# Cross attention of a decoder layer: the value product on the high and low halves of the softmax weights side by side

## The chip, the cores and the metric

The kernel runs on one core of one Trainium2 chip. The metric is the device time in microseconds (us), the median of several runs. TensorE is the matrix engine, VectorE the vector engine, ScalarE the scalar engine, GpSimd (POOL) the fourth, and SyncE (SP) issues the DMAs. In the profile they are PE, DVE, ACT, POOL and SP.

## The reference

One decoder layer on x (8 batches of 224 rows and 512 columns) and a context (8 x 750 x 384). Each of its three parts is followed by a layernorm of x plus the part's output:

```python
x = _layernorm(x + _L0_attn_ref(x, ...))           # self attention, 16 heads of 64, tanh soft clamp
x = _layernorm(x + _L0_xattn_ref(x, ctx_768, ...)) # cross attention
x = _layernorm(x + _L0_ffn_ref(x, ...))            # ternary weights, 8-bit activations

# _L0_xattn_ref, HEADS = 16, DIM_HEAD = 64
q = split_heads(x @ Wq); k = split_heads(context @ Wk); v = split_heads(context @ Wv)
sim = jnp.einsum('bhid,bhjd->bhij', q, k) * SCALE
attn = jax.nn.softmax(sim, axis=-1)
out = jnp.einsum('bhij,bhjd->bhid', attn, v)
out = out.transpose(0, 2, 1, 3).reshape(b, sq, HEADS * DIM_HEAD)
return out @ Wo + bo
```

The change concerns `out = attn x v` of the cross attention: for each batch and head, a product over 750 keys of 224 rows of weights and 64 columns of values.

## The kernel before, in words

**Precision by halves.** Matmuls of float32 data run on fp32r operands. Each operand is split into a high half (the value rounded to fp32r) and a low half (the rest, value minus high), and a product is summed from high x high, high x low and low x high.

**Tiling of the cross attention.** The 16 heads go in two groups of eight (GROUPS = 2). For each group the 8 batches follow one another, so there are 16 steps. In a step the queries (Q0 to Q3) and keys (K00 to K31) are projected for pairs of heads and the values (V00 to V15) for four heads at a time, from the transposed x (XT) and context (CT). For a head h, S are the scores of 112 rows by 750 keys (two heads side by side in banks SA and SB), M the row maxima (DVE, L1618), the exponentials with their row sums (ACT, L1509), R the reciprocals of the sums (DVE, L1623) and N the normalisation of the weights (POOL, L1243).

**From weights to values.** transpose_weights (T, L1392) brings the normalised weights of a head into bank T by three groups of four transposes, so that keys lie on the partitions: six key blocks of 126 (one of 120). For each group weights_hi (ACT, L1515) writes the high half into big_hi, and weights_split (DVE, L1628) the low half into big_lo; the latter frees bank T. weights_view is the place of a group in these tiles, [key, head parity, key block, row]. v_st holds the values of a head as 128 columns, 64 high and 64 low, in an order that changes with the parity of the head.

values (O, L1407) then adds up a head's output in bank O. For each of the six key blocks it runs two products with the same stationary operand, v_st: one with big_hi and one with big_lo as the moving operand, 224 columns each, all twelve into the same 224 columns of the bank. So 64 partitions of the bank hold high values times both halves, and the other 64 hold low values times both halves. lower_values (ACT, L1522) copies the 64 partitions of the low values to the others' place in tmp, and add_values (DVE, L1637) adds the two into o32 and frees the bank. Two heads fill one o32 pair (the even one the first 64 partitions, the odd one the rest). split_output on POOL splits the pair into o_hi (L1248) and o_lo (L1250), and project_out (Y0 and Y1, L1418) multiplies with Wo, after all eight heads. It waits for o_split of pair p before its product 3p+1 of Y0.

**What sets the order.** Each engine works through a list written out by hand (ORDER in tensor, scalar, vector and gpsimd) in which an item with a "+" belongs to the next batch. The engines meet at semaphores: `filled` of a bank is raised by TensorE, `drained` by the last reader. In the stretch around O of TensorE's list: "T3.1 CT01+ O2 T3.2 CT02+ CT10+ S3.0 T4.0 CT11+ O3 T4.1 V00+ V01+ T4.2", and at the turn of the step "T1.1 K30+ K31+ O0+ S2.0+ T1.2 V11+ V12+ T2.0+ V13+ V14+". VectorE's list has there "M6.0 T4.0 CT11+ M7.0 O3 T4.1 R6.0" and "Y1 finish T1.1 K30+ O0+ K31+ M4.0+ T1.2 V11+ M5.0+ V12+"; finish is the bias in the first group and the layernorm in the second. POOL's list has B0 to B3 (split_output of a pair) among the N and the pieces FR, FC and FT of the feed-forward weights, of which FR waits for a DMA. The last step has lists of its own, and further banks (END_UNITS).

Of the kernel before, what the change touches and what calls it, by code (L numbers as in the profile page):

```python
# [14 lines left out]
ALU = mybir.AluOpType  # L15
ACT = mybir.ActivationFunctionType
AX = mybir.AxisListType
F32 = mybir.dt.float32
F32R = mybir.dt.float32r
# [3 lines left out]
P = 128  # L23
BANK = 512
HALF = 64
# [49 lines left out]
def f32(ap):  # L75
    return ap.bitcast(F32)
# [797 lines left out]
def cross_attention(nc, ctx_mem, mem, psum, shared, sa_free, sa_projected, sa_stage_free, ff_scaled, x1, ctx, Wq, Wk, Wv, Wo, bo, acc, x2, ff_held, ff_weights, ff_ternary, ff_scale):  # L874

    B, N, DM = x1.shape
# [4 lines left out]
    NP = HG // 2  # L881
    GC = HG * D
    KC, CC = DM // P, CD // P
    R = N // 2
    J = 126
    JC = -(-S // J)
    J0 = [min(J * j, S - J) for j in range(JC)]
    JL = S - J * (JC - 1)
    JN = [J] * (JC - 2) + [JL, J]
# [21 lines left out]
    def sem(name):  # L911
        return ctx_mem.enter_context(nc.semaphore("ca_" + name))
# [5 lines left out]
    in_late = Map(nc, "ca", mem["late"])  # L918
# [16 lines left out]
    v_st = in_early("v_st", [J, JC, HG, 2 * D], F32R)  # L935
# [2 lines left out]
    k_hi = in_late("k_hi", [P, NP, S], F32R)  # L938
    k_lo = in_late("k_lo", [P, NP, S], F32R)
    pr = in_late("pr", [R, PB, 2, S])  # L940
    big_hi = in_late("big_hi", [P, 2, JC, N], F32R)
    big_lo = in_late("big_lo", [P, 2, JC, N], F32R)
    w_hi.append(in_late("w_hi3", [P, blocks_k[3], GC], F32R))
    w_lo.append(in_late("w_lo3", [P, blocks_k[3], GC], F32R))
    assert in_late.at <= mem["rows"]
# [4 lines left out]
    tmp = in_late("tmp", [P, N])  # L950
    o32 = in_late("o32", [P, 2, N])
# [34 lines left out]
    def slot_of(u, at):  # L986
        return plan_of(at).slot[u]
# [20 lines left out]
    t_hi_done = sem("t_hi_done")  # L1008
    max_done = sem("max_done")
    rec_done = sem("rec_done")  # L1010
    norm_done = sem("norm_done")
    tmp_done = sem("tmp_done")
    o_hi_done = sem("o_hi_done")
    o_split = sem("o_split")
    y_done = sem("y_done")
# [57 lines left out]

        return WORK.index((h, k)) + 1

    def weights_view(t, h, k):

        v = t[0:J, h % 2, :, :]
        if k == 0:
            return v[:, 0:4, 0:R]  # L1080
        if k == 2:
            return v[:, 2:6, R:N]
        return bass.AP(t, v.offset + R, [v.ap[0], (4 * N - R, 2), (N, 2), (1, R)])

    def blocks_view(bank, k):

        v = bank[0:J, 0:4 * R]
        return v.rearrange("s (c j r) -> s c j r", c=2, j=2) if k == 1 else v.rearrange("s (j r) -> s j r", j=4)
# [150 lines left out]
    def gpsimd(pool):  # L1239
# [5 lines left out]
        def split_output(p, at, place):  # L1245
            source = place(f"O{2 * p + 1}", at)
            pool.wait_ge(source.drained, source.nth_drained)
            pool.tensor_tensor(o_hi[:, p, :], o32[:, p % 2, :], zero[:, 0:1].to_broadcast([P, N]), ALU.add).then_inc(o_hi_done, 1)  # L1248
            pool.wait_ge(o_hi_done, at(NP, p + 1))
            pool.tensor_tensor(o_lo[:, p, :], o32[:, p % 2, :], f32(o_hi[:, p, :]), ALU.subtract).then_inc(o_split, 1)  # L1250
# [53 lines left out]
    def tensor(pe):  # L1304
# [90 lines left out]
        def values(h, at, place):  # L1395

            to, source = place(f"O{h}", at), [place(f"T{h}.{t}", at) for t in range(3)]
            pe.wait_ge(to.free, to.nth_free)
            for n, s in enumerate(source):
                if all(s.drained is not later.drained for later in source[n + 1:]):  # L1400
                    pe.wait_ge(s.drained, s.nth_drained)
            if h % VH == 0:
                v = f"V{h // VH}{JC - 1}"
                pe.wait_ge(drained[slot_of(v, at)], drained_count(v, at))
            for j in range(JC):
                for n, ws in enumerate((big_hi, big_lo)):
                    mm = pe.matmul(to.bank[:, 0:N], v_st[0:JN[j], j, h, :], ws[0:JN[j], h % 2, j, :],  # L1407
                                   start=(j == 0 and n == 0), stop=(j == JC - 1 and n == 1))
            mm.then_inc(to.filled, 1)

        def project_out(c, at, place):
# [62 lines left out]
    def scalar(act):  # L1474
# [37 lines left out]
        def weights_hi(h, t, at, place):  # L1512
            source = place(f"T{h}.{t}", at)
            act.wait_ge(source.filled, source.nth_filled)
            act.activation(weights_view(big_hi, h, t), blocks_view(source.bank, t), ACT.Copy).then_inc(t_hi_done, 1)  # L1515

        def lower_values(h, at, place):

            source = place(f"O{h}", at)
            act.wait_ge(source.filled, source.nth_filled)  # L1520
            to = HALF * (h % 2)
            act.activation(tmp[to:to + HALF, :], source.bank[HALF - to:P - to, 0:N], ACT.Copy).then_inc(tmp_done, 1)  # L1522


# [50 lines left out]
    def vector(dve):  # L1575
# [49 lines left out]
        def weights_split(h, t, at, place):  # L1625
            source = place(f"T{h}.{t}", at)
            dve.wait_ge(t_hi_done, at(3 * HG, 3 * h + t + 1))
            dve.tensor_tensor(weights_view(big_lo, h, t), blocks_view(source.bank, t), f32(weights_view(big_hi, h, t)),  # L1628
                              ALU.subtract).then_inc(source.drained, 1)

        def add_values(h, at, place):
            source = place(f"O{h}", at)
            dve.wait_ge(tmp_done, at(HG, h + 1))
            p, p0 = h // 2, HALF * (h % 2)
            if p >= 2 and h % 2 == 0:
                dve.wait_ge(o_split, at(NP, p - 1))
            dve.tensor_tensor(o32[p0:p0 + HALF, p % 2, :], source.bank[p0:p0 + HALF, 0:N], tmp[p0:p0 + HALF, :],  # L1637
                              ALU.add).then_inc(source.drained, 1)

        def add_residual(g, c, at, place):  # L1640
            source = place(f"Y{c}", at)
# [719 lines left out]
```

## Time and profile before

| | |
|---|---|
| median of 3 runs | 1980.3 us (1979.96 to 1980.8) |
| the profiled execution's own time | 1984.88 us |
| its span, first to last instruction | 1982.7 us |
| mean granted TensorE clock | 0.98 |
| self attention | to about 690 us |
| cross attention, 16 steps | about 690 to 1800 us |
| feed-forward | from about 1800 us |

The span is read from the trace of one profiled execution, with time 0 at its first instruction. "us" of an instruction is its own duration; matmuls are pipelined, so that the duration of one overlaps the next, and the distance of starts is what a product takes in a run of them.

### The profile page before, as it was taken

What the parts mean: (1) busy time and instruction counts of PE and PEld (TensorE: products, weight loads), DVE (VectorE), ACT (ScalarE), POOL (GpSimd) and SP (SyncE); (2) the same over time, 40 slices, a digit from 0 to 9 for tenths busy, and PEclk for the clock granted to TensorE, in tenths of its full rate; (3) what the DMA queues carried; (4) which work ended last, traced back from release to release, by engine and by line L of the source; (5) the groups of instructions that cost most, each with busy time, mean ns of one, the idle gap of its engine ahead of it and who ended that gap; (6) DMA issues with size and microseconds to landing.
All of it is one profiled execution on the core that took longest, in us unless ns stands there. A gap on an engine that the chain in (4) does not pass through costs nothing.

```text
span 1982.7 us, 40803 instructions
## 1 busy us (share of the span) xinstructions
PE 1873.9 (95%) x13440; PEld 1581.0 (80%) x13466; DVE 1483.8 (75%) x3358; ACT 1193.2 (60%) x2632; POOL 941.0 (47%) x977
## 2 busy tenths in 40 slices
PE   5999998999998999999999999999999999988997
PEld 3777776777776899999999988899999988975443
DVE  4667666788788777777877766877777787777887
ACT  3676776665666566556656655656555565654664
POOL 0343342344343266675666533556557556340554
PEclk8899998999998999999999999999999999999999
DMA  3321323011113211211221221121121121043211
GB/s 104 125 88 60 110 70 102 29 47 37 37 36 107 85 53 52 72 48 46 72 74 40 74 62 50 47 75 54 49 72 45 49 72 50 17 108 85 63 63 58
DMA packets 90444, 128.10 MB, mean 65 GB/s; under 512 B 32193, under 2 KB 48801, under 8 KB 90385
## 3 DMA queue, kind: packets, MB, share of 16 engines
q1 hardware_dynamic: 85584, 116.88, 19.4%
q10 hardware_dynamic: 3840, 7.34, 1.1%
q0 software_dynamic: 960, 3.15, 0.4%
q8 instruction: 31, 0.51, 0.1%
q14 instruction: 29, 0.23, 0.0%
HBM read 96.36 MB, written 24.69 MB: 61 GB/s over the span
## 4 chain that ended last, share of the span: by engine, by line
PE 64%; DVE 13%; issue 8%; ACT 6%; DMA 4%; POOL 3%; POOLq 0%; SPq 0%; DVEq 0%; ACTq 0%
PE att_ps_P L1358 10%; PE att_ps_P L1348 8%; PE att_ps_O L1407 8%; PE att_ps_T L1392 7%; PE att_ps_SA L1381 6%; PE att_ps_P L1339 4%; PE att_ps_O L1418 4%; PE att_ps_T L423 3%; PE att_ps_P L423 3%; PE att_ps_SB L481 2%; DMA out_dram<-ff_y_out 2%; PE att_ps_P L1330 2%; PE att_ps_SA L450 1%; DVE att_ps_O L678 1%; PE att_ps_T L436 1%
## 5 line engine op out<-in xcount | busy, mean ns | idle before, releaser
L1243 POOL TENSOR_TENSOR ca_pr<-ca_pr,ca_rec 112x750 f32<-112x750 f32 x256 | 366.6, 1448 | 328.5 <-DVE ca_rec L1623 325.6
L1515 ACT ACTIVATE ca_big_hi<-att_ps_T 126x448 fp32r<-126x448 f32 x374 | 203.6, 544 | 133.2 <-PE att_ps_T L1392 130.9
L368 POOL TENSOR_TENSOR sa_p_lo<-sa_pr,sa_p_hi 112x448 fp32r<-112x448 f32 x128 | 148.3, 1171 | 279.7 <-ACT sa_p_hi L567 279.7
L1628 DVE TENSOR_TENSOR ca_big_lo<-att_ps_T,ca_big_hi 126x448 fp32r<-126x448 f32 x374 | 231.7, 620 | 37.2 <-ACT ca_big_hi L1515 28.8
L1392 PE MATMUL att_ps_T<-att_ident,ca_pr 112*126 112x112 f32 x1496 | 210.3, 263 | 7.1 <-DVE ca_big_lo L1628 7.0
L1407 PE MATMUL att_ps_O<-ca_big_hi,ca_v_st 126*128 126x224 f32 x756 | 184.1, 285 | 5.3 <-DVE ca_big_lo L1628 2.7
L1392 PEld LDWEIGHTS att_ps_T<-att_ident,ca_pr 112*126 112x126 f32 x1496 | 160.4, 140 | 33.5 <-issue 18.2
L1407 PE MATMUL att_ps_O<-ca_big_lo,ca_v_st 126*128 126x224 f32 x756 | 178.0, 277 | 0.0
L1358 PE MATMUL att_ps_P<-ca_w_hi,ca_ct_hi 128*126 128x256 f32 x576 | 172.8, 300 | 5.2 <-DVE ca_v_st L1611 4.1
L1358 PE MATMUL att_ps_P<-ca_w_hi,ca_ct_lo 128*126 128x256 f32 x576 | 162.1, 281 | 0.0
L1358 PE MATMUL att_ps_P<-ca_w_lo,ca_ct_hi 128*126 128x256 f32 x576 | 162.0, 281 | 0.0
L1407 PEld LDWEIGHTS att_ps_O<-ca_big_hi,ca_v_st 126*128 126x128 f32 x756 | 147.1, 195 | 5.8 <-issue 3.1
L1407 PEld LDWEIGHTS att_ps_O<-ca_big_lo,ca_v_st 126*128 126x128 f32 x756 | 146.8, 194 | 0.0
L1504 ACT ACTIVATE ca_v_st<-att_ps_P 126x256 fp32r<-126x256 f32 x192 | 73.5, 383 | 114.1 <-PE att_ps_P L1358 114.0
L1348 PE MATMUL att_ps_P<-ca_ct_hi,ca_w_hi 128*128 128x376 f32 x384 | 134.9, 351 | 0.0
L1509 ACT ACTIVATE ca_pr<-att_ps_SA,ca_nmax 112x750 f32<-112x750 f32 x128 | 113.4, 886 | 30.6 <-DVE ca_nmax L1618 30.6
L1618 DVE TENSOR_REDUCE ca_nmax<-att_ps_SA 112x1 f32<-112x752 f32 x128 | 120.0, 938 | 15.6 <-PE att_ps_SA L1381 14.9
L1501 ACT ACTIVATE ca_k_hi<-att_ps_P 128x375 fp32r<-128x375 f32 x128 | 62.0, 484 | 113.8 <-PE att_ps_P L1348 111.7
L1348 PE MATMUL att_ps_P<-ca_ct_lo,ca_w_hi 128*128 128x376 f32 x384 | 128.3, 334 | 0.0
L711 DVE RECIPROCAL sa_sums<-sa_sums 128x224 f32<-128x224 f32 x64 | 97.1, 1537 | 41.2 <-ACT sa_sums L576 41.2
L1348 PE MATMUL att_ps_P<-ca_ct_hi,ca_w_lo 128*128 128x376 f32 x384 | 127.8, 333 | 0.0
L1606 DVE TENSOR_TENSOR ca_k_lo<-att_ps_P,ca_k_hi 128x375 fp32r<-128x375 f32 x128 | 69.8, 545 | 72.1 <-ACT ca_k_hi L1501 70.5
(282 smaller groups left out, 6268.0 us busy)
## 6 DMA issues: line engine op xcount, KB each, us to landing
ca_ctx_in<-in_ctx_dram SPq DMA_DIRECT2D x16, 567.0 KB
sa_xin<-in_x_dram SPq DMA_DIRECT2D x16, 448.0 KB, 3.7
ca_xin<-x SPq DMA_DIRECT2D x16, 448.0 KB, 3.7
ternary<-ca_stage SPq DMA_DIRECT2D x36, 172.0 KB, 1.9
ca_ctx_in<-in_ctx_dram SPq DMA_DIRECT2D x16, 378.0 KB
ca_stage<-in_L_ffn_w_gate_dram SPq DMA_DIRECT2D x12, 344.0 KB, 4.1
ca_stage<-in_L_ffn_w_up_dram SPq DMA_DIRECT2D x12, 344.0 KB, 3.1
ca_stage<-in_L_ffn_w_down_dram SPq DMA_DIRECT2D x12, 344.0 KB, 3.3
```

Of the source, the lines that this page charges most:

```text
L368: pool.tensor_tensor(p_lo[:, h % NB, :], pr[:, h % NB, :], f32(p_hi[:, h % NB, :]), ALU.subtract).then_inc(p_split, 1)
L423: mm = pe.matmul(ps(u)[0:R, :], xs[:, k, c * R:c * R + R], ws[i][:, k, :], start=(n == 0), stop=(n == len(passes) - 1))
L1243: pool.tensor_tensor(w, w, rec[:, h % PB, c:c + 1].to_broadcast([R, S]), ALU.mult).then_inc(norm_done, 1)
L1348: mm = pe.matmul(ps(u, at)[:, 0:SH], ws[:, k, p * P:p * P + P], cs[:, k, a * S1:a * S1 + SH], start=(n == 0), stop=(n == len(todo) - 1))
L1358: mm = pe.matmul(ps(u, at)[0:J, 0:VC], cs[:, k, J0[j]:J0[j] + J], ws[:, k, vh * VC:vh * VC + VC], start=(n == 0), stop=(n == len(todo) - 1))
L1381: mm = pe.matmul(ps(u, at)[0:R, BANK * half:BANK * half + SH], qs[of, p, c * R:c * R + R], ks[of, p, half * S1:half * S1 + SH], start=(n = ...
L1392: mm = pe.transpose(to.bank[0:J, n * R:n * R + R], pr[:, h % PB, c, J0[j]:J0[j] + J], ident[0:R, 0:R])
L1407: mm = pe.matmul(to.bank[:, 0:N], v_st[0:JN[j], j, h, :], ws[0:JN[j], h % 2, j, :], start=(j == 0 and n == 0), stop=(j == JC - 1 and n == 1))
L1509: act.activation(pr[:, h % PB, c, :].rearrange("r (a s) -> r a s", a=2), two_halves(u, at), ACT.Exp, bias=nmax[:, h % PB, c:c + 1], accum_ ...
L1515: act.activation(weights_view(big_hi, h, t), blocks_view(source.bank, t), ACT.Copy).then_inc(t_hi_done, 1)
L1618: dve.tensor_reduce(nmax[:, h % PB, c:c + 1], both, AX.XY, ALU.max, negate=True).then_inc(max_done, 1)
L1628: dve.tensor_tensor(weights_view(big_lo, h, t), blocks_view(source.bank, t), f32(weights_view(big_hi, h, t)), ALU.subtract).then_inc(sourc ...
```

## The change

The two tiles big_hi and big_lo become one, `big`, in which the high and the low half of a key block lie side by side: 448 columns. values runs one product of 448 columns for each key block in place of two of 224, so that the bank holds the sums of the two halves in two places (columns 0 to 223 and 224 to 447). The sum over the halves moves to the reading. lower_values copies the first 224 columns of the low values' partitions only, so the product of low values and low weights, which was part of the sum before, is left out of it. add_values becomes a tensor_reduce on VectorE over pairs of elements 224 apart (a view of 64 x 224 x 2) and no longer adds tmp. tmp is added by a new tensor_tensor on GpSimd, ahead of the split of the pair, with a new semaphore, o_summed. ScalarE, before it writes tmp for an even head, waits until GpSimd has added the pair before.

```diff
-    big_hi = in_late("big_hi", [P, 2, JC, N], F32R)
-    big_lo = in_late("big_lo", [P, 2, JC, N], F32R)
+    big = in_late("big", [P, 2, JC, 2, N], F32R)
...
+    o_summed = sem("o_summed")
...
-    def weights_view(t, h, k):
+    def weights_view(h, k, lo):
-        v = t[0:J, h % 2, :, :]
+        v = big[0:J, h % 2, :, int(lo), :]
         if k == 0:
             return v[:, 0:4, 0:R]
         if k == 2:
             return v[:, 2:6, R:N]
-        return bass.AP(t, v.offset + R, [v.ap[0], (4 * N - R, 2), (N, 2), (1, R)])
+        return bass.AP(big, v.offset + R, [v.ap[0], (8 * N - R, 2), (2 * N, 2), (1, R)])
...
         def split_output(p, at, place):
             source = place(f"O{2 * p + 1}", at)
             pool.wait_ge(source.drained, source.nth_drained)
+            pool.tensor_tensor(o32[:, p % 2, :], o32[:, p % 2, :], tmp[:, :], ALU.add).then_inc(o_summed, 1)
+            pool.wait_ge(o_summed, at(NP, p + 1))
             pool.tensor_tensor(o_hi[:, p, :], o32[:, p % 2, :], zero[:, 0:1].to_broadcast([P, N]), ALU.add).then_inc(o_hi_done, 1)
...
             for j in range(JC):
-                for n, ws in enumerate((big_hi, big_lo)):
-                    mm = pe.matmul(to.bank[:, 0:N], v_st[0:JN[j], j, h, :], ws[0:JN[j], h % 2, j, :],
-                                   start=(j == 0 and n == 0), stop=(j == JC - 1 and n == 1))
+                mm = pe.matmul(to.bank[:, 0:2 * N], v_st[0:JN[j], j, h, :], big[0:JN[j], h % 2, j, :, :].rearrange("s l n -> s (l n)"),
+                               start=(j == 0), stop=(j == JC - 1))
             mm.then_inc(to.filled, 1)
...
         def lower_values(h, at, place):
 
             source = place(f"O{h}", at)
             act.wait_ge(source.filled, source.nth_filled)
-            to = HALF * (h % 2)
+            to, p = HALF * (h % 2), h // 2
+            if p and h % 2 == 0:
+                act.wait_ge(o_summed, at(NP, p))
             act.activation(tmp[to:to + HALF, :], source.bank[HALF - to:P - to, 0:N], ACT.Copy).then_inc(tmp_done, 1)
...
             if p >= 2 and h % 2 == 0:
                 dve.wait_ge(o_split, at(NP, p - 1))
-            dve.tensor_tensor(o32[p0:p0 + HALF, p % 2, :], source.bank[p0:p0 + HALF, 0:N], tmp[p0:p0 + HALF, :],
-                              ALU.add).then_inc(source.drained, 1)
+            both = source.bank[p0:p0 + HALF, 0:2 * N].rearrange("p (l n) -> p n l", l=2)
+            dve.tensor_reduce(o32[p0:p0 + HALF, p % 2, :], both, AX.X, ALU.add).then_inc(source.drained, 1)
```

weights_hi and weights_split write through the new weights_view; nothing else of them changes.

## Rows read from the trace of the kernel before

**Rows 1.** The page, part 1: busy time (share of the span) and count by engine.

```profile
PE 1873.9 (95%) x13440; PEld 1581.0 (80%) x13466; DVE 1483.8 (75%) x3358; ACT 1193.2 (60%) x2632; POOL 941.0 (47%) x977
```

**Rows 2.** Busy time by stretches: us, PE, PEld, DVE, ACT, POOL, PEclk, DMA, GB/s.

```profile
1000.00:1100.00 100.00, 100.00 (x795) 91.92 (x794) 72.80 (x140) 57.89 (x133) 65.41 (x50) 1.00 0.19 58
...
1300.00:1400.00 100.00, 98.98 (x783) 90.80 (x781) 75.23 (x169) 56.88 (x131) 65.54 (x48) 1.00 0.19 60
```

**Rows 3.** Waits of PE, 1100 to 1800 us: total, times, longest; the longest entry.

```profile
PE att_ps_T L1392 <- DVE ca_big_lo L1628: 5.7, 7, 1.0
```

**Rows 4.** Chain of waits in order of time: start, us, what, number of instructions.

```profile
1006.20 3.10 PE att_ps_P L1348 x18
...
1009.68 1.35 PE att_ps_O L1407 x12
...
1016.97 2.14 PE att_ps_P L1358 x18
...
1022.37 2.76 PE att_ps_O L1418 x12
```

**Rows 5.** Timeline, PE: start, duration; first and last of twelve products.

```profile
683.41 0.27 PE L1407 MATMUL att_ps_O<-ca_big_hi,ca_v_st 126*128 126x224 f32 x1
...
684.63 0.28 PE L1407 MATMUL att_ps_O<-ca_big_lo,ca_v_st 126*128 126x224 f32 x1
```

**Rows 6.** Groups of instructions: shapes, count, busy us, mean ns, idle before.

```profile
L1407 PE MATMUL att_ps_O<-ca_big_hi,ca_v_st 126*128 126x224 f32 x756 | 184.1, 285 | 5.3 <-DVE ca_big_lo L1628 2.7 <-DVE ca_o L1637 2.5
...
L1618 DVE TENSOR_REDUCE ca_nmax<-att_ps_SA 112x1 f32<-112x752 f32 x128 | 120.0, 938 | 15.6 <-PE att_ps_SA L1381 14.9
...
L1637 DVE TENSOR_TENSOR ca_o<-att_ps_O,ca_tmp 64x224 f32<-64x224 f32 x126 | 48.9, 388 | 44.8 <-ACT ca_tmp L1522 43.8
...
L678 DVE TENSOR_REDUCE att_ps_O<-sa_sq 112x8 f32<-112x512 f32 x64 | 44.2, 691 | 36.4 <-ACT sa_sq L547 36.2
...
L1250 POOL TENSOR_TENSOR ca_o_lo<-ca_o,ca_o_hi 128x224 fp32r<-128x224 f32 x64 | 43.6, 682 | 5.0
```

**Rows 7.** Timeline around O1, O2 and O3 of a step of the first group.

```profile
1044.71 0.62 DVE L1628 TENSOR_TENSOR ca_big_lo<-att_ps_T,ca_big_hi 126x448 fp32r<-126x448 f32 x1 [0.18 <-ACT ca_big_hi L1515]
...
1049.38 0.61 DVE L1628 TENSOR_TENSOR ca_big_lo<-att_ps_T,ca_big_hi 126x448 fp32r<-126x448 f32 x1
...
1050.16 0.55 PE L1392 MATMUL att_ps_T<-att_ident,ca_pr 112*126 112x112 f32 x4
...
1054.74 0.93 DVE L1618 TENSOR_REDUCE ca_nmax<-att_ps_SB 112x1 f32<-112x752 f32 x1
...
1055.71 0.40 DVE L1637 TENSOR_TENSOR ca_o<-att_ps_O,ca_tmp 64x224 f32<-64x224 f32 x1
...
1056.13 0.62 DVE L1628 TENSOR_TENSOR ca_big_lo<-att_ps_T,ca_big_hi 126x448 fp32r<-126x448 f32 x1
...
1057.14 0.55 PE L1392 MATMUL att_ps_T<-att_ident,ca_pr 112*126 112x112 f32 x4
```

**Rows 8.** Timeline behind the layernorm of a step of the second group.

```profile
1400.08 0.62 DVE L1628 TENSOR_TENSOR ca_big_lo<-att_ps_T,ca_big_hi 126x448 fp32r<-126x448 f32 x1
...
1400.75 0.60 PE L1392 MATMUL att_ps_T<-att_ident,ca_pr 112*126 112x112 f32 x4 [0.83 <-DVE ca_big_lo L1628]
...
1401.07 0.37 DVE L1637 TENSOR_TENSOR ca_o<-att_ps_O,ca_tmp 64x224 f32<-64x224 f32 x1
...
1404.38 0.40 DVE L1611 TENSOR_TENSOR ca_v_st<-att_ps_P,ca_v_st 126x256 fp32r<-126x256 f32 x1
...
1404.90 0.32 PE L1358 MATMUL att_ps_P<-ca_w_hi,ca_ct_hi 128*126 128x256 f32 x1
```

**Rows 9.** Timeline: the last pair's low split, and the tenth product of Y0.

```profile
1021.70 0.67 POOL L1250 TENSOR_TENSOR ca_o_lo<-ca_o,ca_o_hi 128x224 fp32r<-128x224 f32 x1
...
1024.28 0.39 PE L1418 MATMUL att_ps_O<-ca_w_hi,ca_o_hi 128*112 128x512 f32 x1
```

**Rows 10.** Timeline of the last step: the first product of O3.

```profile
1772.98 0.37 PE L1407 MATMUL att_ps_O<-ca_big_hi,ca_v_st 126*128 126x224 f32 x1 [2.54 <-DVE ca_o L1637]
```

More of the change, by code:

```diff
@@ L1514, in weights_hi @@
             act.wait_ge(source.filled, source.nth_filled)
-            act.activation(weights_view(big_hi, h, t), blocks_view(source.bank, t), ACT.Copy).then_inc(t_hi_done, 1)
+            act.activation(weights_view(h, t, False), blocks_view(source.bank, t), ACT.Copy).then_inc(t_hi_done, 1)
         def lower_values(h, at, place):
@@ L1627, in weights_split @@
             dve.wait_ge(t_hi_done, at(3 * HG, 3 * h + t + 1))
-            dve.tensor_tensor(weights_view(big_lo, h, t), blocks_view(source.bank, t), f32(weights_view(big_hi, h, t)),
+            dve.tensor_tensor(weights_view(h, t, True), blocks_view(source.bank, t), f32(weights_view(h, t, False)),
                               ALU.subtract).then_inc(source.drained, 1)
```

## The prediction

> **What bounds the kernel now.** I began with the shares by engine on the page: the matrix engine is busy 95% of the span and the vector engine 75% [rows 1]. An average over stages says little, so the table by stretches came next. In the stretches of the cross attention that were read, matmuls cover 100 and 99 us of 100, while the vector engine works 73 and 75 us [rows 2]. The granted clock is 1.00 there, the 2.4 GHz level. The list of waits of the matrix engine from 1100 us on is nearly empty: its largest entry is 5.7 us in seven waits of at most 1.0 us, for the vector engine's low halves [rows 3]. The chain of waits in order of time is one run of matmuls behind another [rows 4]. So here the matrix engine's pace sets the time. A cheaper product is worth its full saving, as long as no other engine becomes late. What is to be found is the pace of one product, and who becomes late.
>
> **Part 1: the products.** A product's duration in a group row overlaps the next one, so I take the distance between starts. Twelve products of 224 columns start from 683.41 to 684.63 [rows 5]: eleven distances, 0.111 us each. The chain gives the same (1.35 us for x12, 0.1125) and the prices of wider ones: 256 columns 2.14/18 = 0.119, 376 columns 3.10/18 = 0.172, 512 columns 2.76/12 = 0.230 [rows 4]. From 376 to 512 a column costs 0.43 ns, so 448 columns lie at 0.172 + 72 x 0.00043 = 0.203 us. From 224 to 256 columns the step is only 8 ns for 32 columns, so the narrow product pays something that isn't its columns; I take that to be the weight load of 128 columns. Removing one product in two pays it half as often. A head goes from 12 x 0.111 = 1.332 (or 1.35 by the chain) to 6 x 0.203 = 1.218 us: 0.114 to 0.132 saved, and I take 0.12. There are 756 products with the high half into bank O [rows 6] and 12 into bank SB, which is 6 for each of 128 heads. **First term: 128 x 0.12 = -15.4 us** (ends -14.6 and -16.9).
>
> The Trainium skill ("TensorE: Matmul & The Clock Gate", section "Back-to-back issue gap") gives N/2.4 + 2.5 ns for an isolated product. By it two products of 224 columns would take 191.7 ns and one of 448 189.2, so this term would be 768 x 2.5 ns = -1.9 us. The trace disagrees: at 224 columns it has 111 ns where the rule has 96 [rows 5], and at 376 and 512 it has 172 and 230 where the rule has 159 and 216 [rows 4]. The measured prices are used.
>
> **Part 2: the vector engine.** add_values was a sum of 64x224 at 388 ns; it becomes a reduction over 64x448 out of the bank. Reductions in the trace take 691 ns for 512 elements and 938 for 752 [rows 6], which is 1.03 ns for each element, so 448 take 0.625 us: 0.24 more, or 30 us in all on an engine with a quarter of its time free. The trace shows no reduction whose inner step is 224 elements apart, nor one that gives an output for every two elements. Its bounds are 0 (it reads one operand where the sum reads two, of which one is finished early) and +0.7 (every element twice as dear, 1.09 us). I take +0.24, since both known reductions lie on one line.
>
> What matters is where it delays a release that the matrix engine needs soon. A released product starts 0.05 us behind its release (1400.08 + 0.62 against 1400.75) [rows 8]; a larger gap is slack. Going through the order lists I find three places without cover; in the others the vector engine idles 0.4 us or more soon after the head, and the delay is gone.
> - T3.2 behind O2: release 1049.99, start 1050.16 [rows 7], slack 0.12. O2 becomes 0.12 shorter. And of the 0.24 that O1's read adds, the vector engine's idle 0.18 before T2.2 [rows 7] takes up all but 0.06, which no gap takes up until T3.1. 0.18 of lateness against 0.12 of slack: 0.06 to 0.07 is lost, in each step.
> - T4.2 behind O3: between M7.0, O3 and T4.1 the vector engine has no idle time. T4.1's low half ends at 1056.75 and T4.2 starts at 1057.14 [rows 7], slack 0.34. It ends 0.24 later while the products come 0.12 sooner: 0.03 lost.
> - In the second group the layernorm on the vector engine holds T1.2 up by 0.83 us [rows 8], so what O0 saves just before it (0.12) is waited away. O0's own read [rows 8] then delays everything of the backlog: V12's low half ends at 1404.78 and V14 starts at 1404.90 [rows 8], slack 0.07, so 0.17 is lost. This holds in seven steps.
>
> **Second term: 16 x 0.10 + 7 x 0.29 = +3.6 us.**
>
> **Part 3: GpSimd.** Each of 64 pairs gets one more tensor_tensor of 128x224. The nearest row is the low split with 682 ns [rows 6]; the semaphore between the two adds some 0.07. That is 48 us on an engine 47% busy. Behind it wait the splits, and behind them project_out. Its tenth product is the first that needs the last pair: it starts at 1024.28, while the split ended at 1022.37 [rows 9], 1.9 us of slack. The new chain is 0.24 + 0.75 longer and the heads around it shorten by up to 0.24: 1.2 us, so it is covered, and I cost it at nothing. If POOL were held up a further 0.7 us (its weight chunk by DMA stands ahead of it in its queue), it would cost that, at most 16 times. The normalisations queued behind the add wait for reciprocals anyway.
>
> **Part 4: the scalar engine's new wait.** lower_values of an even head waits until GpSimd has added the pair before. Behind it on the engine are the copies of T, which gate everything. Between O3 and O4 its list has twelve other items, and the add starts right behind the vector engine's read. Zero, in exchange for the same POOL delay as above. The copies and the low halves write into the new layout in runs of 112 as before: zero.
>
> **Part 5: the last step.** Its heads have gaps around them: O3 waited 2.54 us for the vector engine's read of O2 [rows 10], which now comes 0.24 later, and some heads run at half clock, where the merged product saves more. I set its net at -0.4 in place of -0.7: +0.3.
>
> **Sum: -15.4 + 3.6 + 0.3 = -11.5 us.** The profiled execution took 1984.9 us (span 1982.7), 4.6 above the median of the runs, and the change doesn't touch that difference: 1973.4 there, and 1968.8 against the median of 1980.3. What a measurement of this kernel can tell from no change is about 0.2%, 4 us.
>
> **The rivals.**
> (a) Everything is covered: the read costs no more than the sum did, or the small slacks aren't used up. Then the first term stands alone, up to -16.9: 1963.4 to 1966. For it: three losses of a few hundredths rest on slacks of the same size. Against it: the seven layernorm waits are real [rows 3]. Chance 0.2.
> (b) The vector engine becomes the bound of the places above. If the reduction takes 1.09 us (+0.7), O1, O2 and O3 lose some 1.1 us a step and O0 0.7 in seven: 18 + 5 = 23 us, less 15.4: about +7, 1987. It decides from +0.56 (a reduction of 0.95 us) on. For it: the inner step is new. Against it: an element costs 1.03 ns in both reductions. Chance 0.06. Halfway, at about 0.8 us, the time would be 1973 to 1977; chance 0.12.
> (c) The wide product costs as much as two narrow ones, 0.222 us, since 0.111 is all streaming. Then the first term is zero, the losses stay small without the shortening, and the time is 1981 to 1984. Against it: 376 and 512 columns bracket 448 and give 0.203. Chance 0.03.
> (d) GpSimd's longer chain reaches project_out in each step: up to 16 x 0.7 = 11 us, which cancels the gain: 1979. For it: a DMA stands ahead in its queue. Against it: 1.9 us of slack. Chance 0.04.
>
> **How the numbers follow.** My forecast has chance 0.55, at 1968.8. Its own bounds (0.114 to 0.132 a head, losses of 2 to 6 us) give 1965 to 1973. The range takes in (a) whole and most of the halfway case of (b): 1962 to 1976.5, which leaves out about 0.15. Faster by over 0.2% (under 1976.3): the forecast, (a) and most of halfway, 0.86. Within: the rest of halfway, (d), part of (c), 0.07. Slower: (b) and part of (c), 0.07.
>
> **What would show it.** The chain has six products in 1.22 us for a head, starts 0.203 apart; 0.19 would favour more gain, 0.22 is (c). The reduction takes 0.62 us with 126 instances, the vector engine is busier by 30 us and GpSimd by 43. The matrix engine's waits for the low halves grow from under 6 us to some 10, in the second group behind the layernorm. I am wrong if the read takes 0.9 us or more, if matmuls wait for o_split, or if the scalar engine's wait for GpSimd shows in the list.

## The result: no gain, 0.3% slower than before

The changed kernel takes **1986.6 us** (median of 8 runs, 1983.3 to 1988.9). The kernel before, on the same chip, takes 1980.1 (8 runs, 1978.0 to 1985.2). The ratio is **1.0029 [1.0018, 1.0040]**. A second set of runs (e8 below) gives 1.0021 [1.0012, 1.0031]. The forecast was 1968.8, so some 18 us are missing. The profiled execution of the changed kernel took 1986.8 us.

### The profile after

The page, part 1, of the changed kernel:

```profile
span 1985.2 us, 39405 instructions
...
PE 1868.8 (94%) x12698; PEld 1546.1 (78%) x12698; DVE 1503.3 (76%) x3358; ACT 1194.9 (60%) x2632; POOL 982.7 (50%) x1041
```

Against [rows 1], TensorE has 742 matmul records fewer (768 by the code; a few records are missing), VectorE is 19.5 us busier and GpSimd 41.7. VectorE's 19.5 is less than the forecast 30, although the read costs its 29.4 us (78.3 against 48.9 [rows 6]): another group became cheaper by 11.9 us, as the fourth line of the groups shows, and one became dearer by some 7, of which more below. The groups (shapes, count, busy us, mean ns, idle before):

```profile
L1408 PE MATMUL att_ps_O<-ca_big,ca_v_st 126*128 126x448 f32 x756 | 183.1, 378 | 4.8 <-DVE ca_o L1641 2.8 <-DVE ca_big L1631 2.0
...
L1641 DVE TENSOR_REDUCE ca_o<-att_ps_O 64x224 f32<-64x448 f32 x126 | 78.3, 621 | 49.5 <-ACT ca_tmp L1525 48.4
...
L1248 POOL TENSOR_TENSOR ca_o<-ca_o,ca_tmp 128x224 f32<-128x224 f32 x64 | 43.3, 677 | 123.2 <-DVE ca_o L1641 123.1
...
L1686 DVE TENSOR_TENSOR ca_res<-ca_res,ca_bias 112x512 f32<-112x512 f32 x16 | 12.7, 835 | 0.0
```

The new operations cost what was forecast. The reduction takes 621 ns (forecast 625) and the add on GpSimd 677 (forecast 682). The fourth line is the bias sum in the first group's `finish`. It took 1578 ns on average before and takes 835 now; nothing of it was changed. I come back to it. Its group before:

```profile
L1683 DVE TENSOR_TENSOR ca_res<-ca_res,ca_bias 112x512 f32<-112x512 f32 x16 | 24.6, 1578 | 0.0
```

The chain of waits of the changed kernel, in order of time:

```profile
1000.49 1.25 PE att_ps_O L1408 x6
...
1003.49 3.10 PE att_ps_P L1350 x18
...
1012.41 1.22 PE att_ps_O L1408 x6
...
1014.01 2.14 PE att_ps_P L1360 x18
```

A head's products are six in 1.22 to 1.25 us, where [rows 4] had twelve in 1.35. The starts of the products lie 0.203 us apart. From a head's first product to the start of what follows it was 1.415 us and is now 1.30. So a head gives 0.115 us, and the first term of the forecast is there: 128 x 0.115 = 14.7 us. The time was lost elsewhere.

### Where it was lost

I took the distance from one step's project_out (Y0) to the next as the length of a step. The table has the median of six steps of the first group, the sum of six steps of the second, and the last step. Here and for all later kernels, these figures are mine, from the starts in each trace.

| | Y0 to Y0, first group | six steps, second group (Y8 to Y14) | last step |
|---|---|---|---|
| before | 69.95 us a step | 426.1 us | 55.6 us |
| after | 69.27 us a step | 436.6 us | 53.3 us |

In the first group, a step became 0.68 us shorter. In the second group, six steps became 10.5 us longer. What lies outside the table (the start, the turn from one group to the next, the feed-forward) and the last step differ by a few us from execution to execution, and the profiled execution of the kernel before was 4.6 us above its median; so the traces differ by 2.4 us in all where the medians differ by 6.5.

The list of TensorE's waits was read in the second group, 1250 to 1760 us. Before the change its longest entry there is the one of [rows 3], 5.7 us in seven waits of at most 1.0. After it (total, times, longest):

```profile
PE att_ps_T L1394 <- DVE ca_big L1631: 14.1, 7, 2.5
PE att_ps_P L1360 <- DVE ca_v_st L1614: 1.4, 2, 0.8
```

These are the seven waits of T1.2 behind the layernorm, the same ones as in [rows 8]. Six of them take 1.9 to 2.5 us, and the seventh, behind the six steps of the table, 0.6. One of the longest in the timeline, with VectorE's instructions ahead of it (start, duration):

```profile
1537.09 0.15 DVE L1788 BATCH_NORM_AGGREGATE ca_mv<-ca_stats 112x2 f32<-112x6 f32 x1
1537.27 0.90 DVE L1790 TENSOR_SCALAR ca_mv<-ca_mv 112x2 f32<-112x2 f32 x1
1538.20 1.36 DVE L1774 TENSOR_SCALAR ca_newton<-ca_mv 112x2 int32<-112x2 int32 x1
1539.60 0.17 DVE L1775 TENSOR_SCALAR ca_rs<-ca_newton 112x2 int32<-112x2 int32 x1
...
1543.15 1.01 PE L1394 MATMUL att_ps_T<-att_ident,ca_pr 112*126 112x112 f32 x4 [2.46 <-DVE ca_big L1631]
```

L1790 (the sum) and L1774 (the shift) are instructions on two elements in each partition. Their neighbour L1775, of the same shape, takes 0.17 us. They take 0.90 and 1.36. What GpSimd did at that time, in the same trace (L1266 is the piece FC2 of its list, L1271 is FT2, L1243 the normalisations):

```profile
1527.14 0.68 POOL L1248 TENSOR_TENSOR ca_o<-ca_o,ca_tmp 128x224 f32<-128x224 f32 x1
...
1529.29 2.51 POOL L1266 TENSOR_SCALAR ca_stage<-ca_stage 128x688 f32<-128x688 f32 x1
1531.88 2.83 POOL L1243 TENSOR_TENSOR ca_pr<-ca_pr,ca_rec 112x750 f32<-112x750 f32 x2
1534.80 1.94 POOL L1271 TENSOR_SCALAR ca_stage<-ca_stage 128x688 bf16<-128x688 f32 x1
1536.70 2.83 POOL L1243 TENSOR_TENSOR ca_pr<-ca_pr,ca_rec 112x750 f32<-112x750 f32 x2
```

The last line is two normalisations of 1.44 us that overlap by a little, N2.1 and N3.1 of the next batch. The first ends at 1538.14 and the second at 1539.53. L1790 ends at 1538.17 and L1774 at 1539.56. Each of the two small instructions on VectorE starts inside a GpSimd instruction and ends just behind its end. Before the change, at the same step:

```profile
1538.11 0.15 DVE L1785 BATCH_NORM_AGGREGATE ca_mv<-ca_stats 112x2 f32<-112x6 f32 x1
1538.29 0.44 DVE L1787 TENSOR_SCALAR ca_mv<-ca_mv 112x2 f32<-112x2 f32 x1
1538.76 0.17 DVE L1771 TENSOR_SCALAR ca_newton<-ca_mv 112x2 int32<-112x2 int32 x1
...
1528.45 2.52 POOL L1264 TENSOR_SCALAR ca_stage<-ca_stage 128x688 f32<-128x688 f32 x1
...
1535.87 2.84 POOL L1243 TENSOR_TENSOR ca_pr<-ca_pr,ca_rec 112x750 f32<-112x750 f32 x2
```

There the two normalisations end at 1538.71. They hold the first small instruction for 0.27 us (it ends at 1538.73), and the second one finds GpSimd idle. With the change GpSimd lies 0.83 us later (1536.70 against 1535.87: the add and its semaphore) and VectorE's layernorm 1.02 earlier (1537.27 against 1538.29: the products). The products did not bring GpSimd forward as well: its run of work starts here with FR2, which waits for a DMA and begins at 1526.33, against 1526.26 before. So the two have moved 1.85 us against each other (1.1 to 1.9 in the six steps), and that is enough for the small chain to meet both normalisations. Over all seven layernorms, by the source lines (ns min/median/max, first and last start), before:

```profile
L1787 DVE TENSOR_SCALAR ca_mv<-ca_mv x7: 170/571/758, 1325.3 to 1751.5; 112x2 f32<-112x2 f32 x7
...
L1771 DVE TENSOR_SCALAR ca_newton<-ca_mv x7: 168/170/171, 1326.0 to 1751.7; 112x2 int32<-112x2 int32 x7
```

and after:

```profile
L1790 DVE TENSOR_SCALAR ca_mv<-ca_mv x7: 170/567/905, 1317.3 to 1754.0; 112x2 f32<-112x2 f32 x7
...
L1774 DVE TENSOR_SCALAR ca_newton<-ca_mv x7: 169/1361/1365, 1317.7 to 1754.2; 112x2 int32<-112x2 int32 x7
```

What lies above 170 ns is time in which VectorE stands still: 2.6 us in all before, 10.2 after (3.1 at L1790 and 7.1 at L1774). It falls on the six steps of the table; in the seventh layernorm, from 1754.0 us on, nothing is held in either trace.

The Trainium skill ("SBUF — State Buffer", section "Who interferes with whom") says that VectorE and GpSimd share a pair of SBUF ports as a lock on the whole instruction: whichever starts first has it, and a VectorE tensor_scalar in a two-port mode is blocked until the other is done. The trace agrees: 0.90 and 1.36 us in place of 0.17, each ending about 0.03 us behind the end of a GpSimd instruction. That it is held is measured; that the ports are the reason is what the Trainium skill says, and no run here can show it. The same section of the Trainium skill says that a VectorE tensor_tensor with both inputs in SBUF meets a GpSimd instruction that reads SBUF, while tensor_reduce never does. For the reductions the trace agrees: of the 256 row maxima of the kernel before (112x752), 49 start inside a normalisation, and none of all takes over 944 ns.

For the bias sum above, with both inputs in SBUF, it agrees in part. The sum takes 0.68 us alone. Before the change 13 of 16 met a normalisation and took 1.5 to 1.9 us; after it two did. But twelve of the sixteen now start inside L1271, a GpSimd instruction that reads SBUF too, and take 0.68 to 0.71 us: there the Trainium skill and the trace differ, and the measurement decides. So it matters which GpSimd instruction it is. These collisions held nothing up: in e3 below they are back (1366 ns on average), and a step of the first group is as long as in the changed kernel.

There is a second loss behind the first. The trace by stretches of 4 us around the wait one step earlier, which was 2.48 us (us, PE, PEld, DVE, ACT, POOL, PEclk, DMA, GB/s), after:

```profile
1464.00:1468.00 4.00, 1.97 (x16) 1.32 (x14) 3.62 (x14) 0.42 (x2) 0.83 (x1) 0.98 0.00 0
1468.00:1472.00 4.00, 3.55 (x17) 3.55 (x18) 3.35 (x7) 1.10 (x3) 0.00 (x0) 0.50 0.42 118
1472.00:1476.00 4.00, 4.00 (x26) 4.00 (x25) 2.31 (x6) 2.01 (x5) 1.44 (x1) 0.66 0.64 200
1476.00:1480.00 4.00, 4.00 (x34) 3.87 (x33) 2.35 (x6) 2.77 (x7) 1.34 (x1) 1.00 0.00 0
```

TensorE waits in the first stretch and to 1468.45 us, and in the next the granted clock is 0.50, the 1.2 GHz level. From 1476 us on it is 1.00 again, the 2.4 GHz level. At the same place before, the row is

```profile
1473.00:1477.00 4.00, 4.00 (x36) 4.00 (x36) 3.73 (x8) 2.38 (x6) 1.14 (x1) 1.00 0.50 164
```

with 36 matmuls in 4 us where the slow stretch has 17 in 3.55. This doesn't follow every long wait. The six steps of the changed kernel, with the wait of T1.2 in each and the mean granted clock of the step:

| step's length, us | 71.65 | 73.35 | 74.82 | 73.33 | 71.77 | 71.69 |
|---|---|---|---|---|---|---|
| wait, us | 1.94 | 2.40 | 2.48 | 2.46 | 2.14 | 2.08 |
| granted clock | 1.00 | 0.98 | 0.95 | 0.98 | 1.00 | 1.00 |

So a wait of that length can cost more than itself. Before the change, with waits of up to 1.0 us, the clock stayed at 1.00 in these steps.

### The profile page after: what moved, and what is told of

Read it like the earlier page. It is cut to its first block, busy times and chain, and to the rows that moved or that the text cites. A ratio compares the mean times of both kernels' runs of the same rounds, so it can differ in the third digit from the quotient of the medians.

```text
span 1985.2 us, 39405 instructions
## 1 busy us (share of the span) xinstructions
PE 1868.8 (94%) x12698; PEld 1546.1 (78%) x12698; DVE 1503.3 (76%) x3358; ACT 1194.9 (60%) x2632; POOL 982.7 (50%) x1041
## 4 chain that ended last, share of the span: by engine, by line
PE 64%; DVE 13%; issue 8%; ACT 7%; DMA 4%; POOL 4%; POOLq 0%; SPq 0%; DVEq 0%; ACTq 0%
PE att_ps_P L1360 10%; PE att_ps_P L1350 8%; PE att_ps_T L1394 8%; PE att_ps_O L1408 7%; PE att_ps_SA L1383 6%; PE att_ps_P L1341 4%; PE att_ps_O L1419 4%; PE att_ps_T L423 3%; PE att_ps_P L423 3%; PE att_ps_SB L481 2%; DMA out_dram<-ff_y_out 2%; PE att_ps_P L1332 2%; PE att_ps_SA L450 1%; PE att_ps_SB L1383 1%; DVE att_ps_O L678 1%
## 5 line engine op out<-in xcount | busy, mean ns | idle before, releaser
L1243 POOL TENSOR_TENSOR ca_pr<-ca_pr,ca_rec 112x750 f32<-112x750 f32 x256 | 364.6, 1442 | 290.8 <-DVE ca_rec L1626 287.9
L1516 ACT ACTIVATE ca_big<-att_ps_T 126x448 fp32r<-126x448 f32 x374 | 203.9, 545 | 141.3 <-PE att_ps_T L1394 138.0
L1631 DVE TENSOR_TENSOR ca_big<-att_ps_T,ca_big 126x448 fp32r<-126x448 f32 x374 | 231.5, 619 | 30.8 <-ACT ca_big L1516 22.8
L1394 PEld LDWEIGHTS att_ps_T<-att_ident,ca_pr 112*126 112x126 f32 x1496 | 161.4, 141 | 53.3 <-DVE ca_big L1631 23.0
L1408 PE MATMUL att_ps_O<-ca_big,ca_v_st 126*128 126x448 f32 x756 | 183.1, 378 | 4.8 <-DVE ca_o L1641 2.8
L1408 PEld LDWEIGHTS att_ps_O<-ca_big,ca_v_st 126*128 126x128 f32 x756 | 135.4, 191 | 12.4 <-DVE ca_o L1641 3.0
L1360 PEld LDWEIGHTS att_ps_P<-ca_w_hi,ca_ct_hi 128*126 128x126 f32 x576 | 110.5, 192 | 14.0 <-issue 8.4
L1621 DVE TENSOR_REDUCE ca_nmax<-att_ps_SB 112x1 f32<-112x752 f32 x128 | 119.1, 930 | 0.0
```

The source lines that it names most:

```text
L1243: pool.tensor_tensor(w, w, rec[:, h % PB, c:c + 1].to_broadcast([R, S]), ALU.mult).then_inc(norm_done, 1)
L1360: mm = pe.matmul(ps(u, at)[0:J, 0:VC], cs[:, k, J0[j]:J0[j] + J], ws[:, k, vh * VC:vh * VC + VC], start=(n == 0), stop=(n == len(todo) - 1))
L1394: mm = pe.transpose(to.bank[0:J, n * R:n * R + R], pr[:, h % PB, c, J0[j]:J0[j] + J], ident[0:R, 0:R])
L1408: mm = pe.matmul(to.bank[:, 0:2 * N], v_st[0:JN[j], j, h, :], big[0:JN[j], h % 2, j, :, :].rearrange("s l n -> s (l n)"), start=(j == 0), ...
L1516: act.activation(weights_view(h, t, False), blocks_view(source.bank, t), ACT.Copy).then_inc(t_hi_done, 1)
L1621: dve.tensor_reduce(nmax[:, h % PB, c:c + 1], both, AX.XY, ALU.max, negate=True).then_inc(max_done, 1)
```

## The experiments

**Theory A:** the add makes GpSimd's chain longer and the products make the rest shorter, so that N2.1 and N3.1 fall on the layernorm's small instructions. **The rival** is what the prediction had in its second term: the dearer read on VectorE makes the low halves late. Each was taken away alone, and A was also brought about in the kernel before.

### e1: the changed kernel without the add

The output lacks low values x high weights, and ScalarE's wait for the add goes with it; for the rest it is the changed kernel.

```diff
-            pool.tensor_tensor(o32[:, p % 2, :], o32[:, p % 2, :], tmp[:, :], ALU.add).then_inc(o_summed, 1)
-            pool.wait_ge(o_summed, at(NP, p + 1))
...
-            if p and h % 2 == 0:
-                act.wait_ge(o_summed, at(NP, p))
```

> The changed kernel without GpSimd's new addition and without ScalarE's wait for it; the low values' term is left out of the result. Theory A (GpSimd runs later against VectorE's layernorm, and its tensor instructions there block VectorE's small tensor_scalars over two inputs from SBUF): the first shift of the layernorm is back to its 0.17 us, the seven waits behind the layernorm are 1.0 us or less each, and the time is 1966 to 1972. Theory B (the dearer read, 621 for 388 ns, eats the gain in VectorE's backlog): the read is still there, so the time stays at 1983 or above.

Measured: 1974.2 us (8 runs, 1971.4 to 1976.9), ratio 0.9967 [0.9956, 0.9977]. The read is as dear as in the changed kernel (621 ns), so 12 us go with the add and the wait for it. The counterpart of L1774 is at 0.17 us again in all seven layernorms. But that of L1790 is still held in six of them, for 3.2 us in all, and the wait list (680 to 1810 us) has

```profile
PE att_ps_T L1392 <- DVE ca_big L1627: 7.3, 8, 1.2
```

The products alone leave the sum of the layernorm inside a normalisation, about as long as before the change. A had expected 1966 to 1972 and waits of 1.0 us or less, and both missed by a little. The waits are 3.3 us above those of e3 below (4.0), which is enough to account for it; it was not tested by itself.

### e2 and e7: the kernel before with one and two more sums on GpSimd

One (e2), in split_output, into a place that is overwritten right after; in e7 the two lines stand twice:

```diff
+            pool.tensor_tensor(o_lo[:, p, :], o32[:, p % 2, :], o32[:, p % 2, :], ALU.add).then_inc(o_spare, 1)
+            pool.wait_ge(o_spare, at(NP, p + 1))
```

> The kernel before with one more GpSimd sum of 128x224 ahead of each split, written to where the low half goes afterwards, and a semaphore behind it; nothing else changes. Theory A: GpSimd is 0.75 us later behind each pair and meets more of the layernorm: 1983 to 1990, with VectorE's shift or sum of the layernorm over 0.5 us in most of the seven steps. Theory B: no change, 1979 to 1982.

> The kernel before with two more GpSimd sums of 128x224 ahead of each split, so that GpSimd is 1.5 us later behind each pair, near the 1.9 us by which it lies later against the matrix engine in the changed kernel. Theory A: VectorE's sum and shift of the layernorm are both stretched, to some 0.9 and 1.4 us, 1987 to 1993. Theory B: no change against the run with one more, 1982 to 1984.

Measured, e2: 1983.1 us (10 runs, 1981.3 to 1984.9), ratio 1.0011 [1.0001, 1.0021]. The layernorm and GpSimd of e2, same step as above:

```profile
1537.10 0.93 DVE L1790 TENSOR_SCALAR ca_mv<-ca_mv 112x2 f32<-112x2 f32 x1
1538.06 0.17 DVE L1774 TENSOR_SCALAR ca_newton<-ca_mv 112x2 int32<-112x2 int32 x1
...
1535.17 2.83 POOL L1244 TENSOR_TENSOR ca_pr<-ca_pr,ca_rec 112x750 f32<-112x750 f32 x2
```

L1790 is now held in six of the seven layernorms (1027 ns on average, 5.1 us in all) up to the end of the second normalisation (1538.00 here); L1774 is free. A part of the shift gives the first part of the collision. TensorE's waits for the low half grow from 5.7 to 8.2 us. The time is at the lower end of A's range and 1.1 us above B's, so by itself it decides little; the held instructions are as A has them.

Measured, e7: 1998.3 us (4 runs, 1997.2 to 2002.7), ratio 1.0085 [1.0066, 1.0104]. Its group line and its waits (680 to 1810 us):

```profile
L1776 DVE TENSOR_SCALAR ca_newton<-ca_mv 112x2 int32<-112x2 int32 x7 | 8.3, 1191 | 0.2
```

```profile
PE att_ps_T L1397 <- DVE ca_big_lo L1633: 14.5, 7, 2.4
...
PE att_ps_O L1423 <- POOL ca_o_lo L1255: 1.1, 3, 0.6
```

With 1.5 us more on GpSimd and no other change, L1774's counterpart has the changed kernel's 1191 ns on average to the digit, and the waits are the changed kernel's 14 us. So the collision needs neither the wide product nor the read. It cost more than the 1987 to 1993 expected of A. Project_out now waits three times for GpSimd's split, 1.1 us in all; that is rival (d) of the prediction, and it begins somewhere between one and two more sums. Much of the rest is the clock, for which A had set nothing. All six waits of T1.2 are 2.34 or 2.35 us here. The four steps whose granted clock is 0.98 take 74.3 us on average, and the two at 1.00 take 72.7. So one fall of the clock behind such a wait costs some 1.7 us, and it comes behind some waits and not behind others of the same length.

### e3 and e9, e4: GpSimd's piece FT2 moved behind N4.0

Nothing is left out. N2.1 and N3.1 of the next batch no longer stand behind FT2's last 1.94 us; e3 and e9 do this in the changed kernel (e9 is e3 once more, with e8), e4 in the kernel before.

```diff
-FR2 B3 FC2 N2.0+ N3.0+ FT2 N2.1+ N3.1+ N4.0+ N5.0+
+FR2 B3 FC2 N2.0+ N3.0+ N2.1+ N3.1+ N4.0+ FT2 N5.0+
```

> The changed kernel with GpSimd's third rounding of the feed-forward weights (1.9 us) moved behind the normalisations of N2.1, N3.1 and N4.0, so GpSimd has less to do while VectorE's layernorm runs. Theory A: the layernorm meets at most one GpSimd instruction, 1966 to 1974. Theory B: 1983 or above.

> The kernel before with the same move, as the control of the run before it. Theory A: the 2.6 us by which the layernorm's sum is stretched there shrink, 1975 to 1980. Theory B: 1979 to 1982.

> The changed kernel with GpSimd's third rounding behind N4.0 again. Theory A: 1968 to 1973, ratio 0.994 to 0.997, the layernorm's shift at 0.17 us in all seven steps. If the first run of it was a lucky one: above 1976.

Measured: **e3 1969.9 us** (5 runs, 1968.9 to 1973.9), ratio **0.9952 [0.9935, 0.9968]**; e9 1972.9 (5 runs, 1971.2 to 1974.8), ratio 0.9955 [0.9941, 0.9968]; e4 1978.2 (10 runs, 1974.2 to 1979.4), ratio 0.9986 [0.9977, 0.9996]. In e3, the same step:

```profile
1522.00 5.63 POOL L1243 TENSOR_TENSOR ca_pr<-ca_pr,ca_rec 112x750 f32<-112x750 f32 x4
1536.44 1.44 POOL L1243 TENSOR_TENSOR ca_pr<-ca_pr,ca_rec 112x750 f32<-112x750 f32 x1 [8.81 <-DVE ca_rec L1626]
1537.96 1.94 POOL L1271 TENSOR_SCALAR ca_stage<-ca_stage 128x688 bf16<-128x688 f32 x1
...
1528.06 0.17 DVE L1790 TENSOR_SCALAR ca_mv<-ca_mv 112x2 f32<-112x2 f32 x1
1528.26 0.17 DVE L1774 TENSOR_SCALAR ca_newton<-ca_mv 112x2 int32<-112x2 int32 x1
```

All four normalisations are done at 1527.63, 0.43 us ahead of L1790. The moved piece runs at 1537.96, between N4.0 and N5.0, where GpSimd had waited 2.18 us for a reciprocal in the changed kernel. By the source line no instance is held:

```profile
L1774 DVE TENSOR_SCALAR ca_newton<-ca_mv x7: 169/169/171, 1317.6 to 1739.0; 112x2 int32<-112x2 int32 x7
```

```profile
PE att_ps_T L1394 <- DVE ca_big L1631: 4.0, 8, 0.6
```

TensorE waits for the low halves for 4.0 us in place of 14.1. In e4 it is 3.0 in place of 5.7. So one edit of the order, which takes nothing away, turns the change from +0.29% into -0.48%. On the kernel before the same edit gives 2.3 us, about the 2.6 us for which its L1787 had been held. The change by itself, with the collision out of both sides, is e3 against e4: 1969.9 - 1978.2 = -8.3 us.

The sums of steps as in the table above:

| | first group, us a step | six steps, second group |
|---|---|---|
| e4 (before, FT2 late) | 69.97 | 423.6 |
| e3 (after, FT2 late) | 69.27 | 421.4 |
| after | 69.27 | 436.6 |

Six steps of the second group lose 15.2 us to the collision. 10.2 us is what VectorE stood still in them. The rest, some 5 us, I put down to the stretches at 1.2 GHz, by the rows above; e5 and e6 below separate the two.

### e5 and e6: the cheap read

The changed kernel (e5), and e3 (e6), with VectorE's sum of before in place of the reduction. High values x low weights are left out of the sum, and the low values' part is counted twice.

```diff
-            both = source.bank[p0:p0 + HALF, 0:2 * N].rearrange("p (l n) -> p n l", l=2)
-            dve.tensor_reduce(o32[p0:p0 + HALF, p % 2, :], both, AX.X, ALU.add).then_inc(source.drained, 1)
+            dve.tensor_tensor(o32[p0:p0 + HALF, p % 2, :], source.bank[p0:p0 + HALF, 0:N], tmp[p0:p0 + HALF, :],
+                              ALU.add).then_inc(source.drained, 1)
```

> The changed kernel with VectorE's read as it was before, a sum over the first 224 columns and tmp at some 388 ns; the product of high values and low weights is left out of the result. GpSimd's addition stays. Theory A (GpSimd runs late against the layernorm): the collisions stay, VectorE's shift is over 1 us in most of the seven steps, 1980 to 1986. Theory B (the dearer read eats the gain): 1968 or less. Both: a step of the first group, 69.27 us in the changed kernel, loses its small waits and is 69.0 to 69.1.

> The same with GpSimd's third rounding moved behind N4.0. What it has over the run with that move alone (1969.9) is the price of the dearer read by itself: by theory A 16 steps of 0.15 to 0.3, so 1965 to 1968; if the read costs nothing at all, 1969 to 1970.

Measured, e5: 1983.3 us (10 runs, 1977.6 to 1989.0), ratio 1.0007 [0.9995, 1.0019]. Its groups and its waits (680 to 1810 us):

```profile
L1640 DVE TENSOR_TENSOR ca_o<-att_ps_O,ca_tmp 64x224 f32<-64x224 f32 x126 | 48.9, 388 | 48.5 <-ACT ca_tmp L1525 47.5
...
L1774 DVE TENSOR_SCALAR ca_newton<-ca_mv 112x2 int32<-112x2 int32 x7 | 8.3, 1190 | 0.2
```

```profile
PE att_ps_T L1394 <- DVE ca_big L1631: 13.4, 7, 2.5
```

The read is at 388 ns again, VectorE has 29 us less to do, and the collision and its waits are all there. The rival falls as the cause of the missing 18 us. What both theories had expected of the first group, 69.0 to 69.1 us a step, missed: it is 69.3.

Its six steps in the second group take 429.3 us against the changed kernel's 436.6. Most of the 7.3 us is not the read's. In e5's trace the granted clock (the third number from the end) is 1.00 over all six, although its waits of T1.2 are 1.8 to 2.5 us long; the changed kernel's has the falls of the table above.

```profile
1312.00:1741.00 429.00, 416.21 (x3109) 376.65 (x3108) 329.03 (x703) 249.54 (x576) 265.97 (x217) 1.00 0.17 51
```

Against e6, which has no collision, e5 loses 9.3 us in six steps, and its VectorE stands still for 9.5. So where the clock stays up, the loss is what VectorE stood still, and the 5 us beyond it in the changed kernel come with the clock. The times of the ten executions of e5 bear this out: the shortest, 1977.6, has a mean granted clock of 0.982, the longest, 1989.0, has 0.977.

Measured, e6: 1972.5 us (5 runs, 1971.6 to 1976.5), ratio 0.9956 [0.9942, 0.9970], with no instance held. A had 1965 to 1968 expected, and that missed; it is above the 1969 to 1970 of a read that costs nothing, too. By the medians the cheap read gives nothing over e3 (0.9952) or e9 (0.9955). By the traces a step of the second group goes from 70.23 us in e3 to 70.00, so the read's price there is 0.23 us, 1.6 us in seven steps; medians scatter by 2 to 3 us (e3 and e9 are the same kernel). In the first group the step is 69.26 against 69.27: nothing. What the prediction took for losses to the read at T3.2 and T4.2 isn't the read's.

### e8: the changed kernel once more

> The changed kernel again, on one chip with the run below, to have both against the same runs of the kernel before. By every theory 1983 to 1989, ratio 1.002 to 1.004.

Measured: 1985.5 us (11 runs, 1983.5 to 1991.9), ratio 1.0021 [1.0012, 1.0031]. Its profile shows the same L1774 (median 1360 ns) and the same waits (1250 to 1760 us):

```profile
PE att_ps_T L1394 <- DVE ca_big L1631: 14.1, 6, 2.5
```

So the sign stands: slower than before, by 0.2 to 0.3%. Beside it e9, the same change with FT2 moved, is faster than both kernels again.

## Why the prediction was wrong

**First term (right).** 0.115 us a head against 0.12 taken; product starts lie 0.203 us apart as interpolated. 14.7 us against 15.4.

**Second term (too small, and in the first group given to the wrong cause).** In the first group I forecast -0.86 us a step and got -0.68. By the first transposes of each group, 0.05 is lost between T3.2 and T4.0 (forecast 0.07). T4.1, right behind O3, loses 0.09, which I hadn't listed, T4.2 loses 0.03 as forecast, and T5.0 another 0.03. All but the last stay with the cheap read (e6), so they are not the read's, and that the forecast 0.07 and 0.03 came near was luck. I put them down to the way round bank T: transposes, ScalarE's high half, VectorE's low half, next transposes. In the changed kernel T4.0 starts at 1049.27, its high half ends at 1050.46 and its low half at 1051.22, and T4.1 starts at 1051.34. When O between them shrinks, that way doesn't. No run tests this by itself. In the second group, with the collision out of both sides, I forecast -0.57 us a step and e3 against e4 has (421.4 - 423.6)/6 = -0.37. The read's price there was 0.23 us where I took 0.17.

**Part 3, GpSimd costed at nothing (the step that failed).** The working priced the add rightly, as 0.75 us more for each pair, and then asked only who waits for GpSimd over a semaphore: project_out, with 1.9 us of slack, and the normalisations, which "wait for reciprocals anyway". The first answer holds: Y0's waits never show, and neither does ScalarE's wait for the add (part 4, right). The second doesn't hold for the four that matter: N2.0 to N3.1 stand behind the last pair's add and start without any wait (1531.88 and 1536.70, before 1531.05 and 1535.87), so they came later by the whole add. Nobody waits for them over a semaphore, yet they hold VectorE. That is what was missed: a GpSimd instruction also holds VectorE without any semaphore. Costed at nothing, it had VectorE stand still for 10.2 us, where it had been 2.6 before; the experiments put 12 us on the add and its wait (e1), and 13 to 17 on where GpSimd's FT2 stands (e9 against e8, e3 against the changed kernel). The rows of before had the sign of it. The time of L1787 was 170/571/758 ns for two elements in a partition, and the bias sum took 1578 ns where the same data shape later took 835. Here an instruction whose duration varied by four times at one shape was being held, and the question is then where its holder will be after the change. In the step shown N3.1 ended 0.4 us behind L1787's start. With a shift of 1.85 us L1787 would end with N2.1, and L1771 would start inside N3.1.

**The rest of the missing time.** Also missed, and following from that: behind a wait of 2.3 to 2.5 us the granted clock can fall from 2.4 to 1.2 GHz, and part of the loss is paid again over the next products, some 5 us in the changed kernel. My condition for being wrong named a read of 0.9 us, a wait for o_split and ScalarE's wait; none of the three happened. The waits for the low halves, forecast at "some 10" us, came to 14.1, and that line was the trail.

**Part 5 (not borne out).** The last step went from 55.6 to 53.3 us, but that is not the change's doing. The profiled execution of the kernel before had a granted clock of 0.91 there (1741 to 1797 us), that of the changed kernel 0.94. In e4, the kernel before with FT2 late, the step is 52.0 us at 0.97, and in e3 52.4 at 1.00. So without the clock the change makes the last step no shorter, where -0.4 was forecast.

**The rivals.** (a) is out: not all was covered, as even e3 against e4 gives 8.3 us and not the 14.7 of the products. (b) named 1987, and that the time came so near is luck: the reduction never took 0.95 us. (c) is out by 0.203 us. (d) didn't happen with one more instruction for a pair, and did with two (e7).

## What to carry to other kernels

When work is added to GpSimd, or anything shifts it against VectorE, look beside the semaphores at what VectorE runs at the time: list VectorE's short tensor_scalars and its sums of two SBUF operands with their minimum and maximum durations, and see which GpSimd instruction ends where the long ones end. If such a chain gates TensorE, move GpSimd's large instructions away from it; here moving one item of a list was worth 13 to 17 us (e9 against e8, e3 against the changed kernel), more than the change itself. And a saving of 0.1 us at each of many places can give less than its sum: here the heads saved 14.7 us, and 8.3 were left with the collision out of both sides.

## What the runs showed of the hardware that I had not expected

- A VectorE tensor_scalar of 112x2 (0.17 us alone) takes up to 1.36 us when it starts within a GpSimd tensor_tensor of 112x750 (1.44 us). It ends within 0.03 us of the other's end, and the next one can be caught by the next instruction.
- A VectorE tensor_tensor of 112x512 with both inputs in SBUF (0.68 us alone) takes up to 1.9 us beside the same GpSimd tensor_tensor, and 0.68 to 0.71 inside a GpSimd tensor_scalar of 128x688.
- The reduction over pairs of elements 224 apart in PSUM costs 621 ns for 64x448, where the line through the two contiguous ones [rows 6] gives 625. Here the stride cost nothing, as the forecast had taken it.
- Behind a wait of TensorE of 2.48 us the granted clock was 0.50 in the next 4-us stretch. Behind waits of 2.34 us it fell in four of six steps (e7), behind waits of 1.8 to 2.5 us in none (e5), and behind those of up to 1.4 us (e2) in none.
